# A MoE router computed with experts on partitions: one change to a one-core Trainium2 kernel

## The reference

```python
logits = x2 @ gate_w.T                      # 512 tokens x 16 experts
scores = jax.nn.sigmoid(logits)
sc = scores + bias_e                        # 4 groups of 4 experts
# the 2 groups with the highest sum of their top two; in them the 4 best experts
topk_w = scores of the 4, divided by their sum, times 2.5
routed = sum over experts of combine[:, e] * relu(x2 @ up_w[e].T)**2 @ down_w[e].T
shared = relu(x2 @ shared_up.T)**2 @ shared_down.T
out = x + routed + shared
```

## Time and profile before

| what | value |
|---|---|
| median of 3 runs | 352.87 us |
| lowest, highest | 352.58, 354.71 us |
| span of the profiled execution | 350.9 us |
| what lies around it, against the median of the runs | 2.0 us |
| mean granted TensorE clock | 0.995 |
| busy: PE, DVE, ACT, POOL | 332.0, 239.4, 190.5, 98.4 us |
| instructions in the trace | 7040 |

### The profile page before, as it was taken

How to read it: one execution, slowest core, us unless ns; L and a number is a source line. 1 busy time by engine, 2 the same in 40 slices (tenths; PEclk the granted TensorE clock), 3 DMA queues, 4 the chain that set the end, 5 groups by cost and what they waited for, 6 DMA issues and landing times.

```text
span 350.9 us, 7040 instructions
## 1 busy us (share of the span) xinstructions
PE 332.0 (95%) x2554; PEld 235.1 (67%) x2554; DVE 239.4 (68%) x475; ACT 190.5 (54%) x428; POOL 98.4 (28%) x114
## 2 busy tenths in 40 slices
PE   6999989999999998999799899999999999999995
PEld 4988756677777755867689789788544444444453
DVE  2885789655489637748975469980556777778486
ACT  2356765525576476466777454302246777777510
POOL 3600400000001311226584140004446865522000
PEclk9899999999999999999999999999999999999999
DMA  7985499986422227018032471799834463321483
GB/s 228 401 336 177 180 370 404 412 282 197 156 99 90 92 91 290 40 45 346 2 121 92 150 270 32 297 375 398 326 104 164 166 205 133 119 96 62 157 323 120
DMA packets 17185, 69.70 MB, mean 199 GB/s; under 512 B 2816, under 2 KB 3328, under 8 KB 14592
## 3 DMA queue, kind: packets, MB, share of 16 engines
q1 hardware_dynamic: 12768, 56.93, 43.2%
q0 software_dynamic: 3520, 11.54, 9.3%
q10 hardware_dynamic: 864, 0.79, 0.7%
HBM read 61.91 MB, written 7.34 MB: 197 GB/s over the span
## 4 chain that ended last, share of the span: by engine, by line
PE 71%; DVE 15%; ACT 7%; issue 4%; DMA 2%; DVEq 0%; POOL 0%; ACTq 0%
PE bank L2068 10%; PE bank L2100 10%; PE bank L1923 8%; PE bank L1606 8%; PE bank L1608 8%; PE bank L1607 8%; PE bank L2037 3%; PE bank L1815 2%; DVE res L1583 2%; DMA raw<-in_wkT 2%; PE bank L1867 2%; PE bank L1772 2%; DVE cT L1296 1%; PE bank L1762 1%; PE bank L2079 1%
## 5 line engine op out<-in xcount | busy, mean ns | idle before, releaser
L1923 PE MATMUL bank<-ring,wT 128*128 128x384 f32 x128 | 44.0, 487 | 0.7 <-ACT wT L898 0.7
L2068 PE MATMUL bank<-WX,xsT 128*32 128x256 f32 (+1 forms) x256 | 36.4, 380 | 0.0
L2100 PE MATMUL bank<-WX,hsT 128*32 128x512 f32 (+1 forms) x128 | 36.2, 595 | 0.0
L692 POOL DMA_INDIRECT xs<-x_rows,from_row x20 | 22.1, 1108 | 48.9 <-DVE to_row L1250 25.2
L1296 DVE TENSOR_TENSOR cT<-ring_T,cT 128x512 fp32r<-128x512 f32 x45 | 30.0, 710 | 6.5 <-ACT cT L756 6.5
L1923 PEld LDWEIGHTS bank<-ring,wT 128*128 128x128 f32 x128 | 23.6, 190 | 14.2 <-ACT wT L898 0.9
L1530 DVE COPY copy<-WX 128x1024 f32 x32 | 21.1, 703 | 13.1 <-PE bank L2100 5.9
L2068 PEld LDWEIGHTS bank<-WX,xsT 128*32 128x32 f32 x256 | 17.1, 110 | 18.8 <-issue 8.4
L756 ACT CAST cT<-ring_T 128x512 fp32r<-128x512 f32 x48 | 27.0, 619 | 4.6 <-PE bank L1608 4.5
L2068 PE MATMUL bank<-copy,xsT 128*32 128x256 f32 x384 | 29.3, 380 | 0.0
L2100 PE MATMUL bank<-copy,hsT 128*32 128x512 f32 x192 | 29.1, 595 | 0.0
(11 more groups left out here) (296 smaller groups left out, 883.4 us busy)
## 6 DMA issues: line engine op xcount, KB each, us to landing
WX<-in_experts SPq DMA_DIRECT2D x16, 1024.0 KB, 6.9
ring_T<-in_ctxT SPq DMA_DIRECT2D x16, 768.0 KB, 7.3
ring<-in_ctx SPq DMA_DIRECT2D x16, 768.0 KB, 5.1
WX<-y_rows SPq DMA_DIRECT2D x4, 1024.0 KB, 8.1
raw<-in_experts SPq DMA_DIRECT2D x3, 1024.0 KB, 5.0
raw<-in_wqT SPq DMA_DIRECT2D x4, 256.0 KB, 5.7
res<-in_x SPq DMA_DIRECT2D x4, 256.0 KB, 8.1
raw<-in_woT SPq DMA_DIRECT2D x1, 1024.0 KB, 5.8
```

What stands on the lines that cost most here:

```text
L692: nc.gpsimd.indirect_dma_start(out=xs[:, s % NXS, :], out_offset=None, in_=x_rows, in_offset=bass.IndirectOffsetOnAxis(ap=from_row[:, s:s ...
L1923: last = mm(bank[B_O][:, 0:TD], wT[:, g % 2, k * P:(k + 1) * P], ring[:, g % RING, k, :], start=(c == 0 and k == 0), stop=(c == NCH - 1 an ...
L2068: last = mm(bank[B_H[g % 2]][q * SLOT:(q + 1) * SLOT, 0:IC * P], xsT[:, g % 2, c * P + q * SLOT:c * P + (q + 1) * SLOT], w, start=c == 0, ...
L2100: last = mm(bank[B_Y[g % 2]][q * SLOT:(q + 1) * SLOT, :], hsT[:, g % 2, m * P + q * SLOT:m * P + (q + 1) * SLOT], w, start=m == 0, stop=m ...
```

## The change

The router is turned around: the gate weights are stationary (high and low part side by side, 32 columns), the tokens move (128 columns), so that the logits of the two parts stand on 32 partitions, one expert each. 8 matmuls in place of 12. ACT copies them to `lgT`; one fp32 matmul with `fold` (two unit matrices on top of each other) adds the two parts and brings the tokens back to partitions. `logits(b)` and `router_copy(b)` are placed by hand. `upper`, `ones`, `r_sel`, `in_row` and `in_group` become fp32r, so that `counts` and `entries` are fp32r matmuls; the weight `cw4` goes into `in_group` as a high and a low part, which makes its rows 60 columns, and `group_entries` adds the two.

```diff
@@ tiles
-        gate_h = sb("gate_h", [P, DC, NE], F32R)
-        gate_l = sb("gate_l", [P, DC, NE], F32R)
+        gate_hl = sb("gate_hl", [P, DC, 2, NE], F32R)
+        fold = sb("fold", [2 * NE, NE])
+        lgT = at("lgT", [2 * NE, 2, P], hw_at)
+        cw_h, cw_l = (at(n, [P, NK], gate_at + 4 * ND + 64 * i, F32R) for i, n in enumerate(("cw_h", "cw_l")))
-        in_row = at("in_row", [P, NK, P], raw_at)
-        in_group = at("in_group", [P, NK, 2 * NG], raw_at + 8192)
+        in_row = at("in_row", [P, NK, P], raw_at, F32R)
+        in_group = at("in_group", [P, NK, 3 * NG], raw_at + 8192, F32R)
-        y_ok = [sem(f"y_ok{b}") for b in range(NB)]
+        y_ok = sem("y_ok")
@@ ScalarE
+            def router_copy(b):
+                act_e.wait_ge(lgT_mm, b + 1)
+                if b >= 2:
+                    act_e.wait_ge(lg_mm, b - 1)
+                copy(lgT[:, b % 2, :], bank[rows_bank(b)][0:2 * NE, 0:P]).then_inc(lgT_ok, 1)
...
+            router_copy(0)
+            unit_copy(7)
             router_exp(0)
-            unit_copy(7)
...
             unit_copy(11)
+            router_copy(1)
             unit_exp(13)
             router_exp(1)
...
+            router_copy(2)
+            relu_half(1, 0)
             router_exp(2)
-            relu_half(1, 0)
             squared_half(1, 0)
...
+            router_copy(3)
             router_exp(3)
@@ VectorE: weights, rows_of_groups, group_entries, small_parts
                 by_place(cw4, r_cw)
+                link(V_.tensor_copy(cw_h[:], cw4[:]))
+                link(V_.tensor_tensor(cw_l[:], cw4[:], f32(cw_h[:]), ALU.subtract))
...
-                V_.tensor_tensor(in_group[:, :, NG:2 * NG], r_eq[:], cw4[:].unsqueeze(2).to_broadcast([P, NK, NG]),
+                V_.tensor_tensor(in_group[:, :, NG:2 * NG], r_eq[:], f32(cw_h[:]).unsqueeze(2).to_broadcast([P, NK, NG]), ALU.mult)
+                V_.tensor_tensor(in_group[:, :, 2 * NG:3 * NG], r_eq[:], f32(cw_l[:]).unsqueeze(2).to_broadcast([P, NK, NG]),
                                  ALU.mult).then_inc(ent_ok, 1)
...
+                link(V_.tensor_copy(s_ent[:], bank[B_POST][:, 0:NG]))
                 V_.tensor_copy(s_cw[:], bank[B_POST][:, NG:2 * NG])
-                link(V_.tensor_copy(s_ent[:], bank[B_POST][:, 0:NG]))
...
+                V_.tensor_tensor(s_cw[:], bank[B_POST][:, 2 * NG:3 * NG], s_cw[:], ALU.add)
...
+                V_.tensor_tensor(fold[:], ident[0:2 * NE, 0:NE], ident[0:2 * NE, NE:2 * NE], ALU.add)
@@ TensorE
             def router(b):
                 pe.wait_ge(xlo_ok, norm_no["last", b] + 1)
+                pe.wait_ge(small_ok, 1)
+                dst = bank[rows_bank(b)]
                 for c in range(DC):
-                    last = split_mm(bank[rows_bank(b)][:, 0:NE], (xT_h[:, c, tok(b)], xT_l[:, c, tok(b)]),
-                                    (gate_h[:, c, :], gate_l[:, c, :]), c == 0, c == DC - 1)
-                last.then_inc(lg_mm, 1)
+                    mm(dst[0:2 * NE, 0:P], gate_hl[:, c, :, :].rearrange("p i e -> p (i e)"), xT_h[:, c, tok(b)], start=c == 0, stop=False)
+                    last = mm(dst[0:NE, 0:P], gate_hl[:, c, 0, :], xT_l[:, c, tok(b)], start=False, stop=c == DC - 1)
+                last.then_inc(lgT_mm, 1)
+
+            def logits(b):
+
+                pe.wait_ge(lgT_ok, b + 1)
+                mm(bank[rows_bank(b)][:, P:P + NE], lgT[:, b % 2, :], fold[:], start=True, stop=True).then_inc(lg_mm, 1)
...
                 if e == 0:
+                    pe.wait_ge(exp_ok, UNITS)
+                if e == 0 and b == 0:
                     pe.wait_ge(rexp_ok, NB - 1)
-                    pe.wait_ge(exp_ok, UNITS)
...
             unit_T(7)
+            logits(0)
...
             unit_sums(2)
+            logits(1)
...
             first_down(0, 1)
+            logits(2)
             first_down(0, 0)
...
-                    up_half(e, 1, m)
+                    up_half(e, 1, m, (lambda: logits(3)) if e == m == 0 else None)
...
-                    last = mm(bank[B_POST][:, 0:2 * NG], in_row[:, q, :], in_group[:, q, :], start=q == 0, stop=q == NK - 1)
+                    last = mm(bank[B_POST][:, 0:3 * NG], in_row[:, q, :], in_group[:, q, :], start=q == 0, stop=q == NK - 1)
```

More of the change, by code:

```diff
@@ L97, in layer_program @@
         earlier = sb("earlier", [P, NE, NE])
-        ones = sb("ones", [P, 1])
+        ones = sb("ones", [P, 1], F32R)
         filled = sb("filled", [P, MORE])
@@ L287, in layer_program @@
         r_exp = small("r_exp", [P, NB, NE])
-        r_sel = small("r_sel", [P, NB, NE])
+        r_sel = small("r_sel", [P, NB, NE], F32R)
         r_pos = small("r_pos", [P, NB, NE])
@@ L580, in _ @@
             nc.gpsimd.memset(mhalf[:], -0.5).then_inc(consts, 1)
-            nc.gpsimd.memset(ones[:], 1.0)
+            nc.gpsimd.memset(f32(ones[:]), 1.0)
             pool.wait_ge(pool_link, 3)
@@ L1182, in weights @@
                 dve.wait_ge(u_lo_pool, 1)
-                link(V_.tensor_tensor(flat(r_w), flat(r_sel), flat(r_sco), ALU.mult))
+                link(V_.tensor_tensor(flat(r_w), f32(flat(r_sel)), flat(r_sco), ALU.mult))
                 link(V_.tensor_reduce(out=r_sum[:], in_=r_w[:], op=ALU.add, axis=AX.X))
@@ L1586, in add_last @@
                 dve.wait_ge(end_mm, b + 1)
-                V_.tensor_tensor(res[:, b, :], res[:, b, :], bank[B_END[b]][:], ALU.add).then_inc(y_ok[b], 1)
+                V_.tensor_tensor(res[:, b, :], res[:, b, :], bank[B_END[b]][:], ALU.add).then_inc(y_ok, 1)
             results_lo(NG - 2)
@@ L1658, in bias_columns @@
                 for t in range(TC):
-                    mm(bank[3][:, 2 * NB + t:2 * NB + t + 1], row_s[:, t * P:(t + 1) * P], ones[0:2, 0:1], start=True, stop=True)
-                mm(bank[3][:, 2 * NB + TC:2 * NB + TC + 1], row_s[:, TD:TD + 1].to_broadcast([2, P]), ones[0:2, 0:1],
+                    mm(bank[3][:, 2 * NB + t:2 * NB + t + 1], row_s[:, t * P:(t + 1) * P], f32(ones[0:2, 0:1]), start=True, stop=True)
+                mm(bank[3][:, 2 * NB + TC:2 * NB + TC + 1], row_s[:, TD:TD + 1].to_broadcast([2, P]), f32(ones[0:2, 0:1]),
                    start=True, stop=True).then_inc(bias_mm, 1)
@@ L1684, in query_constants @@
                 for b in range(NB):
-                    last = mm(bank[3][:, b:b + 1], const_s[:, tok(b)], ones[0:2, 0:1], start=True, stop=True)
+                    last = mm(bank[3][:, b:b + 1], const_s[:, tok(b)], f32(ones[0:2, 0:1]), start=True, stop=True)
                 last.then_inc(c_mm, 1)
@@ L1715, in down, with up_half @@
                 last.then_inc(acc_mm, 1)
-            def up_half(e, h, m):
+            def up_half(e, h, m, between=None):
                 pe.wait_ge(ulo_first, 2 * e + 2)
@@ L1724, in up_half @@
                                     (xT_h[:, c, half(h)], xT_l[:, c, half(h)]), c == 0, c == DC - 1)
+                    if between is not None and c == 1:
+                        between()
                 if m == IC - 1:
@@ L2004, in counts @@
                 sel = r_sel[:].rearrange("p b e -> p (b e)")
+                one = ones[:, 0:1].to_broadcast([P, P])
                 mm(bank[B_A][:, 0:NB * NE], upper[:], sel, start=True, stop=False)
                 for j in range(1, NB):
-                    mm(bank[B_A][:, j * NE:NB * NE], ones[:, 0:1].to_broadcast([P, P]), sel[:, 0:(NB - j) * NE], start=False, stop=j == NB - 1)
+                    mm(bank[B_A][:, j * NE:NB * NE], one, sel[:, 0:(NB - j) * NE], start=False, stop=j == NB - 1)
                 for b in range(NB):
-                    last = mm(bank[B_A][:, NB * NE:(NB + 1) * NE], ones[:, 0:1].to_broadcast([P, P]), sel[:, b * NE:(b + 1) * NE], start=b == 0, stop=b == NB - 1)
+                    last = mm(bank[B_A][:, NB * NE:(NB + 1) * NE], one, sel[:, b * NE:(b + 1) * NE], start=b == 0, stop=b == NB - 1)
                 last.then_inc(cnt_mm, 1)
```

20 lines of the change are left out of this document (11 added, 9 removed).

## The result

| what | before | after |
|---|---|---|
| median | 353.09 us (22 runs) | 354.41 us (22 runs) |
| lowest, highest | 351.75, 354.71 | 352.58, 356.54 |
| ratio of after to before | | 1.0032, interval 1.0018 to 1.0046 |
| span of the profiled execution | 350.9 us | 354.8 us (its own time was 356.54, the highest of the 22) |

What follows compares the result with a forecast made beforehand. Bound: PE and a serial DVE chain meeting at the first gather. Router 2 +0.1, cw_h/cw_l +0.42, third product +0.41, add +0.08 make the index +1.0, landing taken as +0.8: 353.7 us median, range 352.0 to 355.0.

Steps and rivals of the forecast that it cites:

- Two full engines, and the later one decides: From 218.4 to 234 us PE and DVE are both full; the one whose result the other needs last sets the time.
- Router 0.5 us a block, `counts` 8 records, `entries` 16 records, one record for each fp32r product: On PE: router block 1.33 to 0.5 us, counts 0.88 us less, entries 1.74 us less.
- Router 1, -0.2: At router 1 PE gains 0.2 us at most, since unit_sums(2) waits for ACT's unit_copy(11) and logits(1) costs 0.22.
- Router 2: the squares +0.1 though PE is 0.2 earlier: logits(2) stands behind first_down(0, 1), so the exp and ACT's squares of expert 1 come 0.1 us later, to routing.
- cw_h and cw_l +0.42, third product +0.41, the add +0.08: DVE steps added between r_sel and the index; with router 2's 0.1 they make the index 1.0 us later.
- The halving of `entries` is hidden: Shorter entries on PE bring nothing, because DVE is busy with gated and slot_experts until 235.1 us.
- The gather: First gather of rows lands 0.8 us later, between the index (+1.0) and the expert loads (+0.5), and everything behind moves with it.
- the gather hides: Rival: the first gather lands in time after all and PE's 0.8 us saving stands, 352.1 us; chance 0.18.
- the router is slow: Rival: router matmuls of 128 moving columns take 0.11 us each, routing +0.7, index +1.6, 354.5 us; chance 0.16.
- still two records: Rival: fp32r products here are still two records, PE 0.9 us late at the gather, 353.8 us; within the forecast's case.
- the gather collides: Rival: the expert load behind up(3) shares the engines with the later gather, landing +1.3, index +1.0, 355.2 us; chance 0.08.
- The clock: Rival: PE's new 1.5 us wait before down_half drops the granted clock, costing 1.4 us, up to 355.1 us; chance 0.03.

Runs made afterwards that it cites:

- experiment 1: Changed kernel with the weight not split (no cw_h, cw_l or third product) and entries in fp32 again: 353.14 us, 0.9993 of before.
- experiment 5: Changed kernel with eight more linked 16-element subtractions behind cw_l on DVE: 356.27 us, 1.0072 of before.
- experiment 6: Changed kernel with logits(2) placed behind the third of the six matmuls of first_down(0, 1): 353.94 us, 1.0002 of before.
- experiments 3 and 4: slot_experts moved behind group_entries, in the changed kernel (352.94 us, 0.9984 of before) and in the kernel before (353.28 us, 1.0000).
- experiment 3: Changed kernel with slot_experts moved behind group_entries, its first small add kept in front: 352.94 us, 0.9984 of before.
- experiment 10: Changed kernel with the loads of experts 9 and 14 held until the index is there: 354.19 us, 1.0017 of before.
- experiment 7: Changed kernel with eight 512-column matmuls into a free bank ahead of PE's wait for the first gather: 354.20 us, 1.0013 of before.
- experiments 9 to 12: After again, 1.0029; loads of experts 9, 14 behind the index, 1.0017; slot_experts behind group_entries, cw_h/cw_l on GpSimd: old router 0.9964, new router with logits(2) earlier 0.9937.

## Why the prediction was right

The direction and the size held: +0.8 forecast, +0.6 to +1.6 measured, by the path that was named. That the number came so near is in part luck: in the traces the path grew by 1.4 to 1.7 us, nearly twice the forecast, and before's median stands between its quicker and its slower executions. Step by step:

- *Two full engines, and the later one decides.* Shown: experiment 1 gives back 1.7 us of PE work and loses nothing, experiment 5 adds DVE steps and pays.
- *Router 0.5 us a block, `counts` 8 records, `entries` 16 records, one record for each fp32r product.* As forecast, 0.060 us for a matmul of the new shape. The Trainium skill (TensorE: Matmul & The Clock Gate, Back-to-back issue gap) has some 81 ns for 128 moving columns; the trace has 0.060 us with 32 and 16 stationary columns, so its 0.65 us a block was too much and the rows of the trace were the nearer guide.
- *Router 1, -0.2.* Measured -0.14 (17.95 to 17.81). The wait for `hwT_odd` takes its part of the saving, as named; `unit_sums(2)` came 0.50 us nearer where 0.35 was forecast, and logits took back 0.32 where 0.22 was.
- *Router 2: the squares +0.1 though PE is 0.2 earlier.* That is +0.3 over router 2; measured +0.38. The mechanism (the exp waits for the product behind six matmuls, and ACT's and DVE's queues carry it back to back to routing) is shown by experiment 6, which moves that product alone. What I had not weighed is that this wait was avoidable and that the router's gain sat behind it.
- *cw_h and cw_l +0.42, third product +0.41, the add +0.08.* Measured +0.41 to r_more, and +0.88 of 0.91 to the index.
- *The wait for r_sel at `counts`, 0.2 to some 0.6.* 0.64, read as before at the weight load of the first counting matmul.
- *`down_half(0)` waits 1.5 us, PE reaches `up(3)` 0.8 us sooner.* 1.55 and 0.81.
- *The halving of `entries` is hidden.* Shown by experiments 3 and 4 together: it is behind `slot_experts`.
- *The gather: the term that was mis-sized.* I took +0.8 for the landing, between the index (+1.0) and the loads (+0.5). The index moved by 1.14 (router 1 to `to_row`, 50.84 us before and 51.98 after), and the gather took 7.8 to 8.2 us from issue to PE where 7.6 had been read, so the landing moved by 1.4 to 1.7. The landing did not lag behind the issue, as the choice of +0.8 had it, but moved further than it. By experiment 3 it goes with the issue: behind r_sel the index came 1.93 us sooner and PE got its rows 1.3 to 1.6 us sooner, with the loads of experts 5, 9 and 14 where they were. Where the extra 0.2 to 0.6 us of the gather come from is not shown; the load behind `up(3)`, which now stands nearer to it, fits.

The rivals: *the gather hides* fell (PE waits 1.9 to 2.2 us for it); *the router is slow* fell with 0.060 us a matmul; *still two records* fell; *the gather collides* did not come at its size (the gather took at most 0.6 us longer in after, not 1.3), but a smaller collision is left standing, and experiment 10 does not test it. *The clock* happened in one of the two profiled executions of after; as a general cost of the change it isn't shown, and experiment 7 doesn't settle it.

## What to carry to other kernels

Time saved on one engine is worth what the engine's next wait leaves of it: look for that wait first, and price the few small instructions on the other engine that pay for the saving, since linked steps of 16 elements at 0.21 us count in full on a serial chain. When a product becomes early, move what was put in front of its reader as cover (here `slot_experts`), or nothing is gained; the same move was worth nothing while the product was late. And when a result takes a detour over a second small product, place that product by when its reader needs it, not behind the block of long matmuls that was convenient.

## What the runs showed of the hardware

- *The gather's issue is longer while DVE works.* GpSimd's first gather took 1.06 us to issue in every kernel in which DVE ran out of work at the index, and 1.64 us in all five in which `slot_experts` ran beside it; from its issue to PE it then took 8.3 to 9.0 us, against 7.8 to 8.4 in the others with a wait. The timeline of experiment 3, DVE beside that issue (235.47 to 237.11):

```profile
234.96 1.23 DVE L1250 TENSOR_TENSOR r_ended<-row_no,r_end 128x1024 f32<-128x1024 f32 x1
236.22 1.22 DVE L1252 TENSOR_REDUCE s_exp<-r_ended 128x64 f32<-128x1024 f32 x1
```

  The Trainium skill (SBUF — State Buffer, SBUF: two separate sides) says that DVE and GpSimd share a port pair, and that GpSimd cannot write the descriptors of a DMA while DVE runs an instruction in a two-port mode, as a float32 copy within SBUF does. The two instructions here are not of that kind: on the same page of the Trainium skill (Who interferes with whom) a tensor_tensor and a tensor_reduce did not hold a DMA up. The 0.58 us are there all the same; which instruction makes them, and how, was not isolated. They are a part of why the move in experiment 3 did not bring all of its 1.93 us.
- *Executions of one kernel differ in clock.* On the chip of experiments 9 to 12 the executions of before with a mean granted clock of 0.985 took 354.0 to 354.8 us (9 of them), those with 0.995 took 352.6 to 353.1 (4). The mean clock does not order them all: two with 1.000 took 353.3 and 353.7. In the profiles a stretch at half clock lies within 8 to 14 us in eight, within 164 to 170 in four, about 230 and behind the gather in one each; in that of experiment 7 there is none before the last 4 us. The profiled execution of before has 0.995, and its median over more runs was 353.1 to 354.2, by the chip. So the profiled spans of before and of after's second profile differ by 1.5 us (350.9 and 352.4) where the medians on that chip differ by 0.4 (354.04 and 354.40). What sets the level of an execution was not found. Where 1 us is at stake, distances within a trace are the finer measure.
